# A four-layer graph network on one core: constants made inside the embedding, accumulators cleared by two engines, more tiles fetched row by row

## The chip, the cores and the metric

The kernel runs on one core of a Trainium2 chip. The metric is the device time of one execution in microseconds, as the median of several runs; lower is better. The core has TensorE (PE in the profile, PEld for its weight loads), VectorE (DVE), ScalarE (ACT), GpSimd (POOL) and SyncE (SP), which work in parallel and wait for each other by semaphores, and 16 DMA engines that all queues share.

## The reference

A graph has 6,250 nodes with 256 features and 106,250 directed edges, sorted by destination. Four layers follow each other, each on the normalized and rectified features, each added to its input:

```python
h = jnp.maximum(_layernorm(x), 0.0)
x = x + schnet(h, edge_index, edge_weight, edge_attr)   # msg = (h @ w1.T)[src] * filter(edge); sum by dst; two dense layers
h = jnp.maximum(_layernorm(x), 0.0)
x = x + gat(h, edge_index)                              # 8 heads: softmax over each node's in-edges, weighted sum of h[src]
h = jnp.maximum(_layernorm(x), 0.0)
x = x + mean(h, edge_index)                             # (h @ W + b)[src] summed by dst, divided by the degree
h = jnp.maximum(_layernorm(x), 0.0)
x = x + gcn2(h, edge_index)                             # two graph convolutions with batch norms, 64 and 2 wide
```

## The kernel before

The program is a row of stages; each is a `Phase` with its own buffers and semaphores, and at its end all engines meet in a barrier. Stages on nodes (`embed0`, `nodes_schnet`, `nodes_gat`, `nodes_mean`) go over 13 chunks of 512 nodes (4 tiles of 128). Stages on edges (`edges_schnet`, `edges_gat`, `edges_mean`, `edges_gcn`, `edges_pairs`) go over 832 tiles of 128 edges, in groups of four tiles. For each tile POOL issues one indirect DMA that gathers the source rows of its 128 edges from a table in memory; a one-hot matrix `sel` of the destinations within a window of 128 nodes is built; TensorE multiplies the rows by it into PSUM (`psa`), and DVE adds the result to an accumulator `acc` in SBUF, at a column that is read from the list of destinations. Each engine's program is written out in its own block, in the order in which the engine runs it; nothing is reordered.

- **`constants`**, the first stage: SP loads the index columns `src_sb`, `dst_sb` and `base_b`; POOL makes the identity `ident` and the counters; DVE makes `ones`, `eps`, `iota`, `part`, `pair`, and `rel` (destination less the tile's base). Everything ends before the next stage.
- **`embed0`**, the second stage: SP loads the weights `w`, then x by chunks into a ring of four. For each chunk DVE takes `statistics` (`BATCH_NORM_STATS2`, `BATCH_NORM_AGGREGATE`), ACT turns the variance into `rstd`, DVE normalizes (`n_norm`), TensorE transposes (L282) and projects (L329), ACT copies out (`hT`, `O`), POOL stores. `staggered` runs the steps so that in step s DVE takes the statistics of chunk s and normalizes chunk s-1. DVE also clears the accumulator of the next stage, in four pieces behind the statistics of chunks 1 to 4 (L455), and makes the `penalties`, six operations on 832 columns, ahead of chunk 3.
- **`edges_gat`** (attention): 52 iterations of 16 tiles, rows in a ring of three iterations (48 gathers). On ACT each iteration starts with the selections `sel_t` (L1236) and `copy_src` (`l_src_v`, L1283), which waits for all 16 gathers of its iteration. The accumulator has three planes of 6,656 columns; ACT clears them (L1228) behind a wait for all of DVE's setup (`setup`, 4), whose last instruction is `is_last` (L1342). DVE's first `add` waits for `acc_zero`.
- **`edges_mean`**: 208 groups, rows in a ring of eight groups. Of most groups POOL gathers four tiles (L1971). The last tile of some groups comes in one of two other ways: at `looks` (19 groups, every tenth) TensorE looks the rows up in a copy of the table in SBUF (L2096, in four rounds in the groups before); at `by_row` groups the queue of SP or of ACT fetches 128 single rows into `own` (L1919), two buffers for each queue. `asked[g]` is the number of tiles left to POOL. The schedule of `by_row` follows from `BY_ROW`:

```python
first_at, apart = 20, (GROUPS - 24) // BY_ROW
by_row = {g: h for h in range(2) for g in range(first_at + h * (apart // 2), first_at + h * (apart // 2) + apart * BY_ROW, apart)}
```

With 10 it gives each queue 10 groups, 18 apart, from group 20 (SP) and 29 (ACT). SP also loads, between its tiles, the rows from which the one-hots of the look-ups are made (`mixes`, L1940).

## Time and profile before

| | us |
|---|---|
| median of 3 runs | 5339.54 (5337.13 to 5340.34) |
| the profiled execution | 5341.28 |
| its span | 5339.3 |
| PE busy | 4632.9 (87%) |
| DVE busy | 3945.2 (74%) |
| POOL busy | 3383.1 (63%) |
| ACT busy | 1987.0 (37%) |

The span runs from the first to the last instruction that the profiler saw. Busy shares are averages over stages that have different limits, so they don't say what a change inside one stage is worth. Row times start at the span's start. A row "idle before <-releaser" says how long the engine had stood still ahead of the instruction and what ended that; "issue" is idle time for which the profile shows no cause. A row of a queue (SPq) gives the time over which its transfers were issued, not when they landed.

### The profile page before, as it was taken

How to read it: one execution, taken by the hardware profiler on the slowest of the kernel's cores; microseconds unless marked ns; L12 is line 12 of the kernel's file. 1: busy time of each engine (PE TensorE's matmuls, PEld its weight loads, DVE VectorE, ACT ScalarE, POOL GpSimd, SP SyncE). 2: the span in 40 equal slices, each digit the busy share in tenths (PEclk: the TensorE clock that was granted, in tenths of full speed). 3: DMA queues.
4: the chain of work that ended last, by engine and by line, in shares of the span. 5: the costliest groups of instructions: out<-in, count | busy, mean ns of one | idle time of the engine just before them, and what ended most of it. 6: DMA issues, size and time to landing. Idle time of an engine off the chain costs nothing. (4 is left out here: it accounts for less than half of the span.)

```text
span 5339.3 us, 107982 instructions
## 1 busy us (share of the span) xinstructions
PE 4632.9 (87%) x25603; PEld 3568.3 (67%) x25603; DVE 3945.2 (74%) x8645; ACT 1987.0 (37%) x3745; POOL 3383.1 (63%) x3489
## 2 busy tenths in 40 slices
PE   5999999999995888888885488888876899999793
PEld 4888888888775888888884466666655566666431
DVE  5999999999874888888788555555556677777673
ACT  3767666666534655555554200000003000000470
POOL 2677777777516767676640477777764777777473
PEclk8999999999996988888897799999987999999896
DMA  6333333333334555555535533333336111111243
GB/s 198 116 104 103 104 102 106 101 105 103 94 122 126 130 126 125 127 126 126 126 82 160 170 112 112 112 111 110 107 106 168 38 37 39 39 35 29 61 116 108
DMA packets 460843, 563.49 MB, mean 106 GB/s; under 512 B 213296, under 2 KB 331364, under 8 KB 460288
## 3 DMA queue, kind: packets, MB, share of 16 engines
q0 software_dynamic: 153728, 372.39, 25.9%
q1 hardware_dynamic: 292985, 173.79, 12.2%
q10 hardware_dynamic: 13640, 11.88, 0.9%
q8 instruction: 172, 2.82, 0.2%
q14 instruction: 318, 2.61, 0.2%
HBM read 505.12 MB, written 59.42 MB: 106 GB/s over the span
## 5 line engine op out<-in xcount | busy, mean ns | idle before, releaser
L507 POOL DMA_INDIRECT l_rows<-tmp_tab,l_idx x832 | 882.0, 1060 | 377.8 <-issue 252.2
L1217 POOL DMA_INDIRECT l_rows<-tmp_tab,src_sb x832 | 789.7, 949 | 335.0 <-issue 235.8
L1971 POOL DMA_INDIRECT l_rows<-tmp_tab,src_sb x793 | 749.8, 946 | 247.3 <-issue 236.6
L2267 POOL DMA_INDIRECT l_rows<-tmp_tab,src_sb x695 | 656.4, 944 | 235.5 <-issue 202.0
L805 PE MATMUL l_psw<-l_fw,l_ssp 128*128 128x256 f32 x3328 | 763.1, 382 | 0.0
L805 PEld LDWEIGHTS l_psw<-l_fw,l_ssp 128*128 128x128 f32 x3328 | 615.9, 190 | 154.0 <-issue 77.3
L1537 PE MATMUL l_psa<-l_sel,l_rows 128*128 128x128 f32 x3328 | 605.7, 311 | 52.4 <-DVE acc L1437 51.1
L2370 PE MATMUL l_found<-l_tabs,l_hot 128*128 128x384 f32 (+1 forms) x1872 | 650.6, 501 | 0.0
L1537 PEld LDWEIGHTS l_psa<-l_sel,l_rows 128*128 128x128 f32 x3328 | 511.9, 220 | 69.3 <-DVE acc L1437 56.1
L2118 PE MATMUL l_psa<-l_sel,l_rows 128*128 128x128 f32 x3248 | 436.7, 289 | 129.7 <-DVE l_sel L1983 48.6
L1437 DVE TENSOR_TENSOR acc<-acc,l_psa 128x384 f32 x832 | 460.5, 553 | 104.3 <-DVE acc L1430 9.8
L2118 PEld LDWEIGHTS l_psa<-l_sel,l_rows 128*128 128x128 f32 x3248 | 406.7, 200 | 186.6 <-issue 83.3
L2370 PEld LDWEIGHTS l_found<-l_tabs,l_hot 128*128 128x128 f32 x1872 | 347.4, 191 | 251.5 <-issue 66.1
L1993 DVE TENSOR_TENSOR acc<-acc,l_psa 128x256 f32 x832 | 350.0, 421 | 120.0 <-PE l_psa L2118 22.4
L818 PEld LDWEIGHTS l_psa<-l_sel,l_msg 128*128 128x128 f32 x3328 | 408.0, 192 | 15.7 <-issue 1.6
L2096 PE MATMUL l_found<-region,l_hot 128*128 128x512 f32 x950 | 416.1, 588 | 0.0
L818 PE MATMUL l_psa<-l_sel,l_msg 128*128 128x128 f32 x3328 | 412.5, 276 | 1.3 <-DVE acc L725 1.3
L656 ACT ACTIVATE l_mag<-l_psz,l_fb 128x512 f32<-128x512 f32 x416 | 261.7, 679 | 395.6 <-PE l_psz L792 395.6
L2456 ACT ACT_TABLE_LOAD x1 | 1.3, 1283 | 970.6 <-PEq L127 970.6
L1537 PE MATMUL l_psa<-l_sel,l_wx 128*128 128x128 f32 x1664 | 360.9, 303 | 0.0
L725 DVE TENSOR_TENSOR acc<-acc,l_psa 128x256 f32 x832 | 354.3, 426 | 1.7 <-DVE acc L725 0.6
L705 DVE TENSOR_TENSOR l_msg<-l_psw,l_fb 128x512 f32<-128x512 f32 x416 | 288.4, 694 | 89.8 <-issue 84.4
(368 smaller groups left out, 7962.1 us busy)
## 6 DMA issues: line engine op xcount, KB each, us to landing
l_rows<-tmp_tab,src_sb POOLq DMA_INDIRECT x2320
l_edge<-in_edge_t SPq DMA_DIRECT2D x104, 256.0 KB
l_own<-tmp_tab ACTq DMA_DIRECT2D x1280, 1.0 KB
l_own<-tmp_tab SPq DMA_DIRECT2D x1280, 1.0 KB
l_own<-tmp_tab ACTq DMA_DIRECT2D x1280, 0.2 KB
l_own<-tmp_tab SPq DMA_DIRECT2D x1280, 0.2 KB
tmp_x<-n_X SPq DMA_DIRECT2D x39, 512.0 KB
n_X<-in_x SPq DMA_DIRECT2D x26, 512.0 KB
```

The lines of the kernel that those rows point to most:

```text
L507: nc.gpsimd.indirect_dma_start(out=rows[r][:, t, :], out_offset=None, in_=table[:, :], in_offset=bass.IndirectOffsetOnAxis(ap=idx[q][:, j: ...
L725: nc.vector.tensor_tensor(a, a, psa[:, t * D:(t + 1) * D].rearrange("p (k r) -> p k r", k=KH), ALU.add).then_inc(added, 1)
L805: last = nc.tensor.matmul(psw[:, t * D:(t + 1) * D], ssp[b % 2][:, k, t * P:(t + 1) * P], fw2[:, k, :], start=(k == 0), stop=(k == KH - 1))
L818: last = nc.tensor.matmul(psa[:, t * D + k * P:t * D + (k + 1) * P], msg[b % 2][:, t, k * P:(k + 1) * P], sel[b][:, t, :], start=True, sto ...
L1217: nc.gpsimd.indirect_dma_start(out=rows[r][:, j, :], out_offset=None, in_=dram["tab1"][:, :], in_offset=bass.IndirectOffsetOnAxis(ap=sh["s ...
L1437: nc.vector.tensor_tensor(a, a, part, ALU.add).then_inc(added, 1)
L1537: last = nc.tensor.matmul(psa[:, col:col + P], left, sel[c.p][:, j, :], start=True, stop=True)
L1971: nc.gpsimd.indirect_dma_start(out=rows[g % ROWS][:, t, :], out_offset=None, in_=table[:, :], in_offset=bass.IndirectOffsetOnAxis(ap=sh["s ...
L2096: last = nc.tensor.matmul(found[:, k % 2 * 512:k % 2 * 512 + (top - lo) * D].rearrange("p (h n) -> p h n", n=D), hot[n % 2][:, j, :], tabs ...
L2118: last = nc.tensor.matmul(psa[:, at:at + P], left[:, k * P:(k + 1) * P], sel[b][:, t, :], start=True, stop=True)
L2267: nc.gpsimd.indirect_dma_start(out=rows[g % ROWS][:, t, :], out_offset=None, in_=table[:, :], in_offset=bass.IndirectOffsetOnAxis(ap=sh["s ...
L2370: last = nc.tensor.matmul(found_of(n)[:, 0:SPANS[j] * H3].rearrange("p (h n) -> p h n", n=H3), hot[n % BUFS][:, j, :], tabs[:, j:j + (SPAN ...
```

## The change

Three edits. First, the stage `constants` is gone, its work sits inside `embed0`: SP asks for chunk 0 of x first, then `w`; the index columns come in at chunk 6 and `rel` is made ahead of the statistics of chunk 9; `ones`, `iota`, `part`, `pair` ahead of chunk 2; the penalties move from chunk 3 to chunk 6; the accumulator is cleared in 13 pieces, one behind each normalize. Second, in `edges_gat` ACT clears two planes as its first instructions, and DVE clears the third behind its setup. Third, `BY_ROW` in `edges_mean` is 13 instead of 10: 13 groups for each queue, 14 apart, from group 20 (SP) and 27 (ACT).

```diff
@@ embed0, sync
-                sp.dma_start(w[:, :, :], by_half(dram["w1_t"])).then_inc(w_in, 16)
-
                 def step(at):
-                    if isinstance(at(0).n, int) and at(0).n == 2:
+                    if at(0).n == 6:
+                        sp.dma_start(sh["src_sb"][:, :], dram["src_cols"][:, :]).then_inc(cols_in, 16)
+                        sp.dma_start(sh["dst_sb"][:, :], dram["dst_cols"][:, :]).then_inc(cols_in, 16)
+                        sp.dma_start(base_b[:, :], dram["dst_cols"][0:1, :].broadcast_to([P, TILES])).then_inc(cols_in, 16)
+                    if at(0).n == 3:
                         for i in range(3):
                             sp.dma_start(runs[i][:, :], dram["dst_flat"][:, i:i + TILES * P].rearrange("a (p n) -> (a p) n", p=P)
...
                     sp.dma_start(nm.X[r][:, :, :], node_rows(dram["x"], c.n)).then_inc(x_in[r], 16)
+                    if c.n == 0:
+                        sp.dma_start(w[:, :, :], by_half(dram["w1_t"])).then_inc(w_in, 16)
@@ embed0, vector
+                def ranges():
+
+                    dve.wait_ge(made, 1)
+                    nc.vector.memset(sh["ones"][:, :], 1.0)
+                    nc.vector.tensor_copy(sh["iota"][:, :], iota_i[:, :])
+                    nc.vector.tensor_copy(sh["part"][:, :], part_i[:, :])
+                    nc.vector.tensor_scalar(pair_i[:, :], part_i[:, :], 1, None, ALU.logical_shift_right).then_inc(paired, 1)
+                    dve.wait_ge(paired, 1)
+                    nc.vector.tensor_copy(sh["pair"][:, :], pair_i[:, :])
+
+                def relative():
+
+                    dve.wait_ge(cols_in, 48)
+                    nc.vector.tensor_tensor(sh["rel"][:, :], sh["dst_sb"][:, :], base_b[:, :],
+                                            ALU.subtract).then_inc(rel_done, 1)
+
                 def step(at):
-                    if at(0) and isinstance(at(0).n, int) and at(0).n == 3:
+                    if at(0) and at(0).n == 2:
+                        ranges()
+                    if at(0) and at(0).n == 6:
                         penalties()
+                    if at(0) and at(0).n == 9:
+                        relative()
                     if at(0):
                         c = at(0)
                         dve.wait_ge(x_in[c.n % AHEAD], c.n // AHEAD * 16 + 16)
                         nm.statistics(dve, c)
-                        if isinstance(c.n, int) and 0 < c.n < PEEL:
-                            part = NW // (PEEL - 1)
-                            nc.vector.memset(acc[:, :, (c.n - 1) * part:c.n * part], 0.0).then_inc(cleared, 1)
                     if at(1):
                         nm.normalize(dve, at(1))
+                        c = at(1)
+                        part = NW // CHUNKS
+                        nc.vector.memset(acc[:, :, c.n * part:(c.n + 1) * part], 0.0).then_inc(cleared, 1)
@@ edges_gat, scalar
+                for k in range(KH):
+                    last = nc.scalar.activation(acc[:, k, :], sh["iota"][:, 0:1].to_broadcast([P, NW]), ACT.Copy)
+                last.then_inc(acc_zero, 1)
                 act.preload_act_table_set(EXP_LN)
                 act.wait_ge(setup, 4)
-                for k in range(PLANES):
-                    last = nc.scalar.activation(acc[:, k, :], sh["iota"][:, 0:1].to_broadcast([P, NW]), ACT.Copy)
-                last.then_inc(acc_zero, 1)
@@ edges_gat, vector
+                for k in range(KH, PLANES):
+                    nc.vector.memset(acc[:, k, :], 0.0).then_inc(tail_zero, 1)
                 dve.wait_ge(setup, 4)
...
                         dve.wait_ge(acc_zero, 1)
+                        dve.wait_ge(tail_zero, PLANES - KH)
@@ edges_mean
-    BY_ROW, PERIOD, FIRST, SLOTS = 10, 10, 20, 8
+    BY_ROW, PERIOD, FIRST, SLOTS = 13, 10, 20, 8
@@ bass_gnn_stack
-        constants(nc, dram, sh)
```

How DVE's instructions stand in the first chunks of the embedding before (`n_stats` and `n_mv` belong to statistics, `n_norm` to the normalize, `acc` is the accumulator of the next stage, the rows from L437 on are the penalties):

```order
L246 BN_AGGR n_mv<-n_stats 128x2 x4
L455 MEMSET acc 128x2x1664
L253 TENSOR_SCALAR n_norm<-n_X,n_mv,n_rstd 128x256 x4
L242 BN_STATS n_stats<-n_X 128x6 x4
L246 BN_AGGR n_mv<-n_stats 128x2 x4
L455 MEMSET acc 128x2x1664
L253 TENSOR_SCALAR n_norm<-n_X,n_mv,n_rstd 128x256 x4
L437 TENSOR_TENSOR n_base_r<-n_runs,n_base_r 128x832
L439 CAST n_rel_b<-n_base_r 128x832
L441 TENSOR_TENSOR n_cut<-n_runs 128x832
```

and at the same place now, from the statistics of chunk 1 on:

```order
L245 BN_AGGR n_mv<-n_stats 128x2 x4
L252 TENSOR_SCALAR n_norm<-n_X,n_mv,n_rstd 128x256 x4
L447 MEMSET acc 128x2x512
L419 MEMSET ones 128x128
L420 CAST iota<-n_iota_i 128x128
L421 CAST part<-n_part_i 128x1
L422 TENSOR_SCALAR n_pair_i<-n_part_i 128x1
L424 CAST pair<-n_pair_i 128x1
L241 BN_STATS n_stats<-n_X 128x6 x4
L245 BN_AGGR n_mv<-n_stats 128x2 x4
L252 TENSOR_SCALAR n_norm<-n_X,n_mv,n_rstd 128x256 x4
L447 MEMSET acc 128x2x512
```

The memset stands behind the normalize and is a third of its old size; the penalties are three chunks further on.

ACT at the start of attention before, from the stage's entry to the first selections and the copy of the gathered source values (one wait for DVE's setup stands behind the table load):

```order
L1225 ACT_TABLE_LOAD
L1228 ACTIVATE acc<-iota 128x6656 x3
L1236 ACTIVATE l_sel_t<-l_rel_b,l_minus 128x512
L1241 ACTIVATE l_sel_t<-l_sel_t 128x512
L1236 ACTIVATE l_sel_t<-l_rel_b,l_minus 128x512
```

and now:

```order
L1222 ACTIVATE acc<-iota 128x6656 x2
L1224 ACT_TABLE_LOAD
L1232 ACTIVATE l_sel_t<-l_rel_b,l_minus 128x512
L1237 ACTIVATE l_sel_t<-l_sel_t 128x512
L1232 ACTIVATE l_sel_t<-l_rel_b,l_minus 128x512
```

Two of three clears stand ahead of the load and of the wait; the third is now DVE's.

POOL in the mean layer before, groups 20 to 29 (x3 is a group of which the last tile comes another way):

```order
L1971 DMA l2_rows4<-tmp_tab2,src_sb 128x256 x3
L1971 DMA l2_rows5<-tmp_tab2,src_sb 128x256 x3
L1971 DMA l2_rows6<-tmp_tab2,src_sb 128x256 x4
L1971 DMA l2_rows7<-tmp_tab2,src_sb 128x256 x4
L1971 DMA l2_rows0<-tmp_tab2,src_sb 128x256 x4
L1971 DMA l2_rows1<-tmp_tab2,src_sb 128x256 x4
L1971 DMA l2_rows2<-tmp_tab2,src_sb 128x256 x4
L1971 DMA l2_rows3<-tmp_tab2,src_sb 128x256 x4
L1971 DMA l2_rows4<-tmp_tab2,src_sb 128x256 x4
L1971 DMA l2_rows5<-tmp_tab2,src_sb 128x256 x3
```

and now, groups 20 to 28:

```order
L1970 DMA l2_rows4<-tmp_tab2,src_sb 128x256 x3
L1970 DMA l2_rows5<-tmp_tab2,src_sb 128x256 x3
L1970 DMA l2_rows6<-tmp_tab2,src_sb 128x256 x4
L1970 DMA l2_rows7<-tmp_tab2,src_sb 128x256 x4
L1970 DMA l2_rows0<-tmp_tab2,src_sb 128x256 x4
L1970 DMA l2_rows1<-tmp_tab2,src_sb 128x256 x4
L1970 DMA l2_rows2<-tmp_tab2,src_sb 128x256 x4
L1970 DMA l2_rows3<-tmp_tab2,src_sb 128x256 x3
L1970 DMA l2_rows4<-tmp_tab2,src_sb 128x256 x4
```

ACT's first tile moves from group 29 to group 27; over the stage POOL issues 787 gathers instead of 793.

## Rows read from the trace of the kernel before

**Rows 1.** Groups of instructions by line: busy us, mean ns | idle us before, releasers

```profile
L1217 POOL DMA_INDIRECT l_rows<-tmp_tab,src_sb x832 | 789.7, 949 | 335.0 <-issue 235.8 <-PE l_psa L1537 90.2 <-POOLq L147 9.0
...
L1971 POOL DMA_INDIRECT l_rows<-tmp_tab,src_sb x793 | 749.8, 946 | 247.3 <-issue 236.6 <-POOLq L147 5.9 <-PE l_psa L2118 4.9
```

**Rows 2.** Timeline from the start: start us, us, instruction [idle before <-releaser]

```profile
0.73 0.41 SPq L348 DMA_DIRECT2D src_sb<-in_src_cols  x1
...
6.27 1.03 DVE L375 TENSOR_TENSOR rel<-dst_sb,const_base_b 128x832 f32<-128x832 int32 x1 [4.54 <-DMA const_base_b<-in_dst_cols]
...
9.29 1.01 SPq L416 DMA_DIRECT2D n_X<-in_x  x2
...
13.27 1.41 DVE L242 BATCH_NORM_STATS2 n_stats<-n_X 128x6 f32<-128x256 f32 x4 [5.98 <-DMA n_X<-in_x]
...
15.61 1.41 DVE L242 BATCH_NORM_STATS2 n_stats<-n_X 128x6 f32<-128x256 f32 x4 [0.41 <-DMA n_X<-in_x]
```

**Rows 3.** Timeline, embedding, chunks 1 to 4, DVE

```profile
28.47 1.02 DVE L437 TENSOR_TENSOR n_base_r<-n_runs,n_base_r 128x832 int32<-128x832 int32 x1
...
33.16 1.40 DVE L242 BATCH_NORM_STATS2 n_stats<-n_X 128x6 f32<-128x256 f32 x4
...
38.48 1.20 DVE L253 TENSOR_SCALAR n_norm<-n_X,n_mv,n_rstd 128x256 f32<-128x256 f32 x4
...
42.16 2.83 DVE L455 MEMSET acc<- 128x3328 f32 x1 [0.64 <-issue]
```

**Rows 4.** Timeline, start of the layer after: a memset beside gathers

```profile
4080.94 1.34 DVE L2320 MEMSET l_dst_l<- 128x1536 int32 x1 [0.27 <-issue]
...
4081.81 0.94 POOL L2267 DMA_INDIRECT l_rows<-tmp_tab,src_sb  x1 [0.30 <-issue]
```

**Rows 5.** Timeline, embedding, chunks 5 to 12

```profile
54.88 1.04 PE L282 MATMUL n_psT<-ident,n_norm 128*128 128x128 f32 x8
...
74.04 1.60 DVE L253 TENSOR_SCALAR n_norm<-n_X,n_mv,n_rstd 128x256 f32<-128x256 f32 x4 [0.89 <-ACT n_rstd L264]
...
85.18 1.04 PE L282 MATMUL n_psT<-ident,n_norm 128*128 128x128 f32 x8
```

**Rows 6.** Timeline, start of the attention layer (gathers 16, 32 and 48)

```profile
1650.53 17.03 ACT L1228 ACTIVATE acc<-iota 128x6656 f32<-128x6656 f32 x3 [12.54 <-DVE l_is_last L1342]
...
1657.88 0.95 POOL L1217 DMA_INDIRECT l_rows<-tmp_tab,src_sb  x1 [0.30 <-issue]
...
1673.81 0.29 ACT L1283 ACTIVATE l_src_v<-l_rows 128x128 f32<-128x128 f32 x1
...
1677.86 0.95 POOL L1217 DMA_INDIRECT l_rows<-tmp_tab,src_sb  x1 [0.30 <-issue]
...
1688.55 0.31 ACT L1283 ACTIVATE l_src_v<-l_rows 128x128 f32<-128x128 f32 x1
...
1697.89 0.95 POOL L1217 DMA_INDIRECT l_rows<-tmp_tab,src_sb  x1 [0.30 <-issue]
...
1706.83 0.31 ACT L1283 ACTIVATE l_src_v<-l_rows 128x128 f32<-128x128 f32 x1
...
1728.96 0.31 ACT L1283 ACTIVATE l_src_v<-l_rows 128x128 f32<-128x128 f32 x1 [0.22 <-issue]
```

**Rows 7.** Timeline, mean layer: SP queue, and TensorE at the first fetched tile

```profile
3046.97 63.58 SPq L1919 DMA_DIRECT2D l_own<-tmp_tab  x128
...
3112.73 63.57 SPq L1919 DMA_DIRECT2D l_own<-tmp_tab  x128
...
3112.41 2.90 PE L2118 MATMUL l_psa<-l_sel,l_rows 128*128 128x128 f32 x12 [6.76 <-DMA l_own<-tmp_tab]
```

**Rows 8.** Timeline, end of the mean layer

```profile
3958.08 2.05 PE L2118 MATMUL l_psa<-l_sel,l_rows 128*128 128x128 f32 x16 [0.54 <-DVE l_sel L1983]
...
3981.61 0.94 POOL L1971 DMA_INDIRECT l_rows<-tmp_tab,src_sb  x1 [0.30 <-issue]
...
3984.40 2.02 PE L2118 MATMUL l_psa<-l_sel,l_rows 128*128 128x128 f32 x16 [1.45 <-issue]
```

More of the change, by code:

```diff
@@ L43 @@
 NP = CHUNKS * CN
-PEEL = 5
 PAD_DST = 6300
@@ L463, in _ @@
                 act.preload_act_table_set(EXP_LN)
+                act.wait_ge(eps_done, 1)
                 def step(at):
@@ L483, in step @@
                         c = at(1)
+                        if c.n == 0:
+                            pe.wait_ge(w_in, 16)
                         pe.wait_ge(nm.hT_done, c.n + 3)
```

57 lines of the change are left out of this document (16 added, 41 removed).

## Prediction

> **What bounds the kernel now.** The program is a row of stages with a barrier after each, so a microsecond saved inside a stage reaches the end whole, unless the same stage gives it back. The chain that ended last only tells of the last stage; I therefore read each of the three stages that the change touches by itself: first the groups by line for who waits for whom, then the timeline around each edit.
>
> Mean layer: GpSimd (POOL) issues 793 gathers, 749.8 us busy plus 247.3 us idle in front of them, of which only 4.9 us were spent waiting for TensorE to free a buffer [rows 1]. POOL never really waits: 1.25 us per gather set the length of the layer. At its end this is plain: TensorE starts a group 1.85 us after that group's last gather was issued (3981.61 + 0.94 to 3984.40) and then waits for the next [rows 8]. Attention layer: the same instruction, 832 times, but with 90.2 us of waiting for `psa` matmuls (57 waits) [rows 1]. POOL needs 16 x 1.25 = 20.0 us for an iteration, an iteration takes somewhat more: the compute engines set the pace, POOL has some 8% to spare. Embedding: from chunk 5 to chunk 12 the transposes start at 54.88 and 85.18, 4.33 us per chunk [rows 5], while VectorE (DVE) has idle time; ahead of that DVE's memsets and penalties stretch the chunks [rows 3].
>
> **Part 1, constants inside the embedding.** What goes: the stage `constants`. Its first transfer is issued at 0.73, its last DVE instruction ends at 6.27 + 1.03 = 7.30, and the first rows of x are asked for at 9.29 only [rows 2]. Now they are the first transfer of the program. It stands behind the one barrier that the transfer at 0.73 stood behind, and five semaphore increments of POOL that no row shows; their cost lies between nothing and the whole step from 7.30 to 9.29, 2.0 us. I take 0.4, as most of that step is the end of a stage, which is gone: x is asked for at 1.1 (0.73 to 2.7), 8.2 us earlier. Chunk 0 lands 4.0 us after it is asked for (13.27 - 9.29), chunk 1 after 6.3 (15.61 - 9.29) [rows 2]; the weights now stand between them instead of ahead, half a us more, so statistics of chunk 1 start at 7.9.
>
> The DVE work changes too. Four memsets of 2x1664 become thirteen of 2x512. A row gives 2.83 us for 3,328 elements, and an idle gap of 0.64 us ahead that nothing released [rows 3]; a memset of 1,536 has 1.34 and 0.27 [rows 4]. The gap grows with the size, so I count it as memset: 3.47 and 1.61, a slope of 1.04 ns per element, which gives 1.61 - 512 x 0.00104 = 1.08 us for 1,024. By the durations alone it would be 0.87. The Trainium skill ("VectorE: DVE Perf Modes", section "Zero memsets can be issued as uint32 (trn2)") says that a memset takes one cycle per element whatever its type; at the 0.96 GHz of its specifications that is an estimate of 3.47 us for 3,328, so by that rule the trace's duration is short by just the gap and the two together agree. For thirteen memsets the rule makes 13.9 us, the durations alone 11.3.
>
> From statistics of chunk 1 to transposes of chunk 5 it was 54.88 - 15.61 = 39.3 us [rows 2, 5]. Take out four memsets (13.9), put in five small ones (5.4) and the five small operations on iota and part (0.9: the penalties' six operations on 832 elements take 33.16 - 28.47 = 4.7 us [rows 3], and these have 128 elements or fewer): 31.7. The penalties stay in this stretch, three chunks later. TensorE now has less slack in the stretch, whose early matmuls are slower, so I add 1.4: transposes of chunk 5 at 7.9 + 31.7 + 1.4 = 41.0 (bounds 39.6 and 43). From there on two paces compete. TensorE's is 4.33. DVE's is 42.16 - 0.64 - 38.48 = 3.04 without a memset [rows 3], 4.12 with it, and 4.52 where the normalize takes 1.60 instead of 1.20 [rows 3, 5], as it does in all steady chunks, where POOL issues a store beside it. Seven chunks at 4.33 to 4.52 and once the subtraction of `rel` (1.03): 31.3 to 32.7. I take 32.1: transposes of chunk 12 at 73.1, against 85.18. All behind them (last projection, stores) is as before. Part 1: **-12.1 us**, bounds -8 (only the earlier start) and -14. The transfers of src, dst and base go in at chunk 6; `rel` is needed by chunk 9's step, over 12 us later, three times what chunk 0 needed to land. That cover hides them; without it DVE would stand for some 4 us.
>
> **Part 2, accumulators of attention.** Before, ScalarE (ACT) first waits until DVE's setup is over and starts three clears at 1650.53, which take 17.03 us; its first selections follow at 1667.5 and `src_v` of iteration 0 at 1673.81 [rows 6]. Now ACT does two planes (2 x 5.7 us) while DVE does its setup, ended by 1650.5, and DVE clears the third plane behind it: 6,656 elements, 6.9 us by the slope, until 1657.5, with nothing queued behind it on DVE but scans that wait for `src_v`. So ACT is free 16.5 us earlier, and `src_v` of iteration 0 could run at 1657.2. But it needs the gathers of its iteration, and POOL's start doesn't move. The 16th, 32nd and 48th gather are issued by 1658.83, 1678.81 and 1698.84 [rows 6]; each lands 1.85 us later [rows 8], so `src_v` can't run before 1660.7, 1680.7 and 1700.7. It ran at 1673.81, 1688.55 and 1706.83: the gain shrinks from 13.1 to 7.9 to 6.1. Iteration 3 came 22.1 us after that (1728.96 [rows 6]), its gathers pass every 20.0: compute is then the slower again and keeps the 6.1. With a TensorE that has its full clock a bit earlier, 6.5. Part 2: **-6.5 us**; bounds -3 (gathers that land late) and -8.5.
>
> Would the memset slow the gathers? Beside the memset at 4080.94 the gather at 4081.81 took 0.94 us [rows 4], as it does without one; I count nothing. A rule of the Trainium skill speaks against this ("SBUF — State Buffer", "Who interferes with whom"): DVE and GpSimd share a port pair as an exclusive lock, and a DVE operation in a two-port mode keeps POOL from writing gather descriptors.  The same page leaves one-input operations outside the two-port modes free of the lock, which by that rule is this case; the trace agrees.
>
> **Part 3, 13 row-fetched tiles on each queue.** Six gathers fewer on POOL: 6 x 1.25 = 7.5 us, if the rows are there. SP needs from one tile's first row to the next tile's 3112.73 - 3046.97 = 65.8 us, 63.6 of it row transfers [rows 7]; with a second one-hot load in the turn 0.45 more. Before, a tile was due on each queue every 18 groups, some 86 us. Now it is every 14 groups: 56 tiles less 3.4 that aren't gathered, 52.6 x 1.25 = 65.8. SP is exactly as fast as it must be. Its first tile was late, TensorE waited 6.76 us until 3112.41, 1.9 us behind the last row [rows 7]; from then on SP stays as late (12 turns of 65.8 plus 3 extra loads: last tile 3112.4 + 791 = 3903.4). So TensorE reaches that tile's group at least 7 us behind the gathers, more than before. Twenty groups follow, at 5.0 us by POOL (4 x 1.25) and 2.05 + 0.54 = 2.6 by TensorE without look-ups [rows 8]; the last seven or so have none, enough to catch up some 15 us. Buffers are eight groups deep, so POOL isn't stopped. ACT's turns are one us shorter than SP's. Part 3: **-7.0 us**, bounds -2 and -7.5.
>
> **Sum.** -12.1 - 6.5 - 7.0 = -25.6. The profiled execution took 5341.28 us (span 5339.3), so the changed one would take 5315.7 in such an execution; the median of before is 1.7 lower, and so is my number: 5314.
>
> **Rivals.**
> - *Attention gives it back.* If the memset of 6.9 us holds up POOL's gathers, the 48th is issued at 1705.7 and `src_v` of iteration 2 can't run before 1707.6, later than its old 1706.83: part 2 is gone, 5314 + 6.5 = 5320.5. For it: that `src_v` has no slack behind the gathers [rows 6]. Against: the gather beside a memset [rows 4]. (The page rule that would bring it about is the port lock of "SBUF — State Buffer" in the Trainium skill, if the memset ran in a two-port mode.) With half of part 1 missing as well, because DVE's 4.52 and late x chunks rule the embedding, 5324. Chance 0.17.
> - *Two parts out of three come to nothing*: gain under 10.7 us, 5329 to 5350. That needs, say, the mean layer to end no earlier, since TensorE doesn't catch up behind SP's last tile, and attention as above. Chance 0.07.
> - *SP becomes the bound of the mean layer*: the one that ends slower. A turn of 65.8 us has no slack; from the point where it is longer than 65.8 + 15/12 = 67 us each further us costs 12. At 70 us (row transfers at 0.53 us instead of 0.50, for instance because ACT's queue now issues all the time) it is +36 against -7.5: 5358. Against: 63.6 us for SP's 128 rows was measured while ACT was issuing too. Chance 0.04.
> - *More than forecast*: embedding at TensorE's pace and the start at 0.73, attention 8.5: under 5307. Chance 0.08.
>
> My forecast (5307 to 5320) has 0.64. Within 0.2% (10.7 us, about what a measurement of this kernel can tell from no change) is the second rival and a slice of others: 0.08; slower 0.04; faster 0.88. The range 5306 to 5325 leaves out the two middle rivals' far ends and the slow one.
>
> **What would show it.** Right: first statistics near 5 us, transposes of chunk 12 near 73, the first gather of the first edge stage some 12 us earlier; ACT's first selection in attention 16 us earlier relative to the stage's first gather and the last `src_v` 6 to 7 us earlier; 787 gathers in the mean layer, which is 7 us shorter, with waits of TensorE for `own` every 14 groups. Wrong: POOL waiting for `psa` in the mean layer, SP turns over 67 us, gathers stretched beside the memset at the start of attention, or a DVE step over 4.6 us in the embedding.

## The result, and the profile after

The changed kernel takes **5300.02 us** (5299.47 to 5301.71, 3 runs) against 5339.54: ratio 0.9928, 95% interval 0.9914 to 0.9941. Forecast were 5314.0, range 5306 to 5325. Sign and two of three sizes were right (parts 1 and 3), that of part 2, the attention layer, was not, and the time lies below the range. Measured once more, in five runs beside ten of before, the ratio was 0.9935 (0.9921 to 0.9948), 5301.75 against 5336.49: 35 to 40 us faster, where 25.5 were forecast.

Where the microseconds came from, by the first and last instruction of each stage in the two profiled executions (shift of that instruction's start against before, us):

| up to | shift | of it in this stage | forecast |
|---|---|---|---|
| transposes of the embedding's chunk 12 | -14.3 | -14.3 | -12.1 |
| last add of the first edge stage | -16.7 | -2.4 | 0 |
| first gather of attention | -17.2 | -0.4 | 0 |
| last add of attention | -34.4 | **-17.3** | -6.5 |
| first gather of the mean layer | -33.8 | +0.7 | 0 |
| last add of the mean layer | -41.4 | -7.6 | -7.0 |
| last add of the program | -40.6 | +0.8 | 0 |

The miss is the attention layer. The groups by line answer to [rows 1]: six gathers fewer in the mean layer, still without a wait for TensorE that matters; in attention POOL waits 69.6 us for `psa` instead of 90.2.

```profile
L1213 POOL DMA_INDIRECT l_rows<-tmp_tab,src_sb x832 | 791.5, 951 | 315.4 <-issue 236.8 <-PE l_psa L1536 69.6 <-POOLq L146 9.0
...
L1970 POOL DMA_INDIRECT l_rows<-tmp_tab,src_sb x787 | 744.1, 945 | 246.0 <-issue 234.0 <-POOLq L146 6.1 <-PE l_psa L2117 5.9
```

The timeline of the embedding, which answers to [rows 2, 3, 5]:

```profile
1.36 0.44 SPq L376 DMA_DIRECT2D n_X<-in_x  x1
5.49 1.41 DVE L241 BATCH_NORM_STATS2 n_stats<-n_X 128x6 f32<-128x256 f32 x4 [3.98 <-DMA n_X<-in_x]
7.70 1.41 DVE L241 BATCH_NORM_STATS2 n_stats<-n_X 128x6 f32<-128x256 f32 x4 [0.28 <-DMA n_X<-in_x]
...
15.76 0.91 DVE L447 MEMSET acc<- 128x1024 f32 x1 [0.16 <-issue]
16.59 1.34 DVE L241 BATCH_NORM_STATS2 n_stats<-n_X 128x6 f32<-128x256 f32 x4
...
38.84 1.10 PE L281 MATMUL n_psT<-ident,n_norm 128*128 128x128 f32 x8 [3.66 <-DVE n_norm L252]
39.77 5.31 PE L328 MATMUL n_psO<-n_w,n_hT 128*128 128x256 f32 x16
44.91 1.04 PE L281 MATMUL n_psT<-ident,n_norm 128*128 128x128 f32 x8
45.79 3.62 PE L328 MATMUL n_psO<-n_w,n_hT 128*128 128x256 f32 x16
...
70.89 1.04 PE L281 MATMUL n_psT<-ident,n_norm 128*128 128x128 f32 x8
```

x is asked for at 1.36 and the statistics of chunk 1 start at 7.70 (forecast 1.1 and 7.9). A memset of 1,024 elements shows as 0.91 with 0.16 of idle "issue" ahead (forecast 1.08 together). Transposes of chunk 5 start at 38.84, 2.2 us earlier than forecast; from there to chunk 12 it is 32.05 us (forecast 32.1). The first of these seven steps takes 6.07 us: behind its wait of 3.66 us TensorE projects at a granted clock of 0.68 (5.31 us for what takes 3.62 at 1.00). The other six take TensorE's 4.33 each, and `rel`, made at 49.35, delays none of them.

The start of the attention layer, which answers to [rows 6]:

```profile
1619.57 11.39 ACT L1222 ACTIVATE acc<-iota 128x6656 f32<-128x6656 f32 x2 [18.78 <-PEq L146]
...
1627.16 1.36 POOL L1213 DMA_INDIRECT l_rows<-tmp_tab,src_sb  x1 [0.30 <-issue]
...
1634.23 5.61 DVE L1340 MEMSET acc<- 128x6656 f32 x1 [1.34 <-issue]
...
1637.78 0.95 POOL L1213 DMA_INDIRECT l_rows<-tmp_tab,src_sb  x1 [0.30 <-issue]
...
1644.53 0.31 ACT L1279 ACTIVATE l_src_v<-l_rows 128x128 f32<-128x128 f32 x1 [5.15 <-DMA l_rows<-tmp_tab,src_sb]
...
1664.62 0.31 ACT L1279 ACTIVATE l_src_v<-l_rows 128x128 f32<-128x128 f32 x1 [7.06 <-DMA l_rows<-tmp_tab,src_sb]
...
1684.86 0.31 ACT L1279 ACTIVATE l_src_v<-l_rows 128x128 f32<-128x128 f32 x1 [4.26 <-DMA l_rows<-tmp_tab,src_sb]
...
1704.84 0.31 ACT L1279 ACTIVATE l_src_v<-l_rows 128x128 f32<-128x128 f32 x1 [3.49 <-DMA l_rows<-tmp_tab,src_sb]
...
1724.75 0.31 ACT L1279 ACTIVATE l_src_v<-l_rows 128x128 f32<-128x128 f32 x1 [2.41 <-DMA l_rows<-tmp_tab,src_sb]
```

As far as `src_v` the mechanism is the forecast one: it now waits for gathers, 2.0 us behind the last of each iteration (forecast 1.85), and DVE's memset (5.61 and 1.34 of gap, forecast 6.9 together) slows no gather: 0.95 beside it. It is beside DVE's setup, some us earlier, that gathers take 1.36. But at `src_v` the wait for gathers doesn't stop at iteration 2: 1704.84 and 1724.75 are still 20 apart. From `src_v` of iteration 2 to that of iteration 8 the windows read, before and then after (columns: stretch; us; busy time of PE, PEld, DVE, ACT, POOL; granted clock; DMA share; GB/s), with iterations 10 to 51 as second row:

```profile
1706.83:1834.49 127.66, 111.43 (x853) 107.83 (x854) 104.56 (x229) 75.91 (x206) 93.81 (x100) 0.90 0.54 131
1880.30:2764.76 884.46, 762.63 (x5823) 736.89 (x5824) 716.05 (x1559) 519.99 (x1396) 611.89 (x647) 0.89 0.52 125
```

```profile
1684.86:1805.74 120.88, 103.29 (x817) 99.69 (x817) 100.84 (x223) 75.83 (x204) 91.32 (x97) 0.93 0.55 135
1853.16:2729.72 876.56, 753.99 (x5824) 728.37 (x5825) 715.25 (x1559) 518.83 (x1396) 614.34 (x649) 0.90 0.52 126
```

By `src_v` the gain is 5.6 us at iteration 2 (counted from the end of the 16th gather; 6.1 forecast), and it seems to grow by 6.8 in the next six iterations. But `src_v` is ACT's, and ACT can run ahead of TensorE: the first window before holds 853 matmuls and the one after only 817. TensorE takes the `src_v` of an iteration with one matmul, `val_ps`. Those of iterations 2 and 8, and the windows between the two, before:

```profile
1713.69 0.33 PE L1475 MATMUL l_val_ps<-ident,l_src_v 128*128 128x128 f32 x1
...
1840.17 0.33 PE L1475 MATMUL l_val_ps<-ident,l_src_v 128*128 128x128 f32 x1
```

```profile
1713.69:1840.17 126.48, 110.25 (x853) 106.65 (x852) 104.60 (x228) 75.90 (x205) 92.26 (x98) 0.91 0.53 131
```

and after:

```profile
1685.22 0.33 PE L1474 MATMUL l_val_ps<-ident,l_src_v 128*128 128x128 f32 x1 [0.42 <-ACT l_src_v L1279]
...
1812.70 0.33 PE L1474 MATMUL l_val_ps<-ident,l_src_v 128*128 128x128 f32 x1
```

```profile
1685.22:1812.70 127.48, 110.25 (x852) 106.61 (x852) 105.50 (x230) 76.20 (x206) 96.40 (x103) 0.91 0.55 134
```

Before, TensorE took `src_v` of iteration 2 only 6.9 us after it ran (1713.69 against 1706.83), as it was busy with earlier iterations; now it waits for it and takes it at once. So TensorE is 12.2 us earlier there, not 5.6. From there to iteration 8 it has the same work at the same granted clock and takes 127.5 us instead of 126.5: it gains nothing in these iterations. What changes in them is ACT's lead over TensorE: it grows from 0.4 to 7.0 us now and was 6.9 and 5.7 us before. Against the end of the 16th gather TensorE is 9.1 us earlier at iteration 1, 12.2 at 2, 11.0 at 3, 11.1 at 8 and 10.8 at 10.

So the layer gained in two places: 10.8 us up to iteration 10, all of it there by iteration 2, and 7.6 in the 41 later iterations, in which nothing was changed. The first 16 gathers took 0.8 longer, as they do in profiles without part 2 too, and the end of the layer 0.4.

In the mean layer SP is as fast as it must be: turns of 65.4 to 66.1 us, and TensorE waits for the fetched rows in six places, 38.8 us in all, without stopping POOL. SP's queue and TensorE, answering to [rows 7]:

```profile
3081.98 63.44 SPq L1918 DMA_DIRECT2D l_own<-tmp_tab  x128
3147.61 63.36 SPq L1918 DMA_DIRECT2D l_own<-tmp_tab  x128
...
3081.81 2.90 PE L2117 MATMUL l_psa<-l_sel,l_rows 128*128 128x128 f32 x12 [9.56 <-DMA l_own<-tmp_tab]
```

### The profile page after: what moved, and what is told of

It reads as the page before. It is cut to its first block and busy times, and to the rows that moved or that the text cites. A ratio compares the mean times of both kernels' runs of the same rounds, so it can differ in the third digit from the quotient of the medians.

```text
span 5299.7 us, 110332 instructions
## 1 busy us (share of the span) xinstructions
PE 4618.3 (87%) x25603; PEld 3553.1 (67%) x25603; DVE 3948.1 (74%) x8655; ACT 1979.7 (37%) x3744; POOL 3379.1 (64%) x3483
## 3 DMA queue, kind: packets, MB, share of 16 engines
q1 hardware_dynamic: 293759, 174.19, 12.1%
## 5 line engine op out<-in xcount | busy, mean ns | idle before, releaser
L503 POOL DMA_INDIRECT l_rows<-tmp_tab,l_idx x832 | 883.5, 1062 | 375.5 <-issue 253.1
L1536 PE MATMUL l_psa<-l_sel,l_rows 128*128 128x128 f32 x3328 | 598.9, 308 | 55.4 <-DVE acc L1436 52.8
L2117 PE MATMUL l_psa<-l_sel,l_rows 128*128 128x128 f32 x3224 | 429.9, 287 | 144.0 <-DVE l_sel L1982 49.9
L1536 PEld LDWEIGHTS l_psa<-l_sel,l_rows 128*128 128x128 f32 x3328 | 504.3, 217 | 72.5 <-DVE acc L1436 58.5
L2117 PEld LDWEIGHTS l_psa<-l_sel,l_rows 128*128 128x128 f32 x3224 | 399.1, 198 | 202.2 <-DVE l_sel L1982 91.8
L1992 DVE TENSOR_TENSOR acc<-acc,l_psa 128x256 f32 x832 | 349.7, 420 | 123.7 <-PE l_psa L2117 25.3
L721 DVE TENSOR_TENSOR acc<-acc,l_psa 128x256 f32 x832 | 342.9, 412 | 1.7 <-DVE acc L721 0.6
```

The source lines that it names most:

```text
L503: nc.gpsimd.indirect_dma_start(out=rows[r][:, t, :], out_offset=None, in_=table[:, :], in_offset=bass.IndirectOffsetOnAxis(ap=idx[q][:, j: ...
L1536: last = nc.tensor.matmul(psa[:, col:col + P], left, sel[c.p][:, j, :], start=True, stop=True)
L1992: nc.vector.tensor_tensor(a, a, p, ALU.add).then_inc(added, 1)
L2117: last = nc.tensor.matmul(psa[:, at:at + P], left[:, k * P:(k + 1) * P], sel[b][:, t, :], start=True, stop=True)
```

## Experiments

Two theories for attention. A: the clears are worth 17 us, fixed. B: they are worth about 10, and the rest is where TensorE's dips to the low clock fall. The expectations count iterations at `src_v`, and so does the text below unless it names TensorE: "it. 2 to 8" is the time between the `src_v` of these iterations, "0 to 10" counts from the end of the 16th gather, and a dip iteration is one of iterations 10 to 50 that took under 23 us at a granted clock below 0.9 (those above are turns of the loop and, rarely, an iteration with a longer stretch at the low clock).

**One part at a time.** The kernel before with one of the three parts, and the changed kernel without part 2. The edits are the three hunks of the change, each by itself.

> The kernel before with part 1 alone (constants inside the embedding, 13 memsets). Theory A (each part has a fixed gain, and the 17 us of the attention layer belong to the clears): 14 us less than before up to the first edge stage, nothing anywhere else, 5325. Theory B (the clears bring about 10 us, and the remaining 7 to 8 us of the attention layer, like 2.5 us of the first edge stage, come from where TensorE's clock dips fall, which any shift of the start changes): also 14 at the start, but the first edge stage and the attention layer each differ by some us from their length before, with either sign; 5315 to 5333.

> The kernel before with part 2 alone (ACT clears two planes first, DVE the third). Theory A: 17 us, all of it in the attention layer, 5322. Theory B: 10 us are there by iteration 9, as in the changed kernel, with the iterations 2 to 8 at POOL's 20.0 us; what comes behind iteration 9 is another number than the changed kernel's 7 to 8 us: 5324 to 5332.

> The kernel before with part 3 alone (13 fetched tiles on each queue). Both theories: the mean layer is 7.0 to 7.5 us shorter, nothing before it moves; 2 us may be given back or gained in the stages behind it, 5331 to 5334.

> The changed kernel with the clears of the attention layer as before (all three on ACT behind the setup). Theory A: 17 us more than the changed kernel, 5317; the attention layer has its old length to within 1 us. Theory B: the attention layer is shorter or longer than in the kernel before by some us although nothing in it is changed, and the total lies 8 to 20 us above the changed kernel, 5308 to 5320.

Measured beside 23 runs of before at 5338.06: part 1 alone 5323.22 (ratio 0.9974, 0.9963 to 0.9985), part 2 alone 5328.94 (0.9982, 0.9973 to 0.9991), part 3 alone 5331.70 (0.9989, 0.998 to 0.9998), parts 1 and 3 5315.64 (0.9962, 0.9949 to 0.9976). That is -14.8, -9.1, -6.4; part 2 comes out at 9 us alone and at some 14 on top of the others. The intervals of the two overlap (5 to 14 for the first; the second is a difference of two programs, each known to some 7 us), so the times don't show that they differ. A falls: 17 us lies outside the first. B agrees with these times, though one expectation of A came true as well: without part 2 the layer has its old length (1167.5 for 1168.1). Two more things: the first edge stage, untouched and unshifted in the profiles of parts 2 and 3 alone, is 3.0 and 2.8 us shorter in them than in the profile before, so its -2.4 is no effect of the change. And the embedding has more than one outcome: of eleven profiles with the same new embedding the last transpose starts at 70.5 to 71.7 in five and at 73.4 to 73.8 in six, by two waits for `rstd`, of at most 1.3 us in the five and of 1.6 to 2.1 in the six; before it is 85.9. The forecast of -12.1 is that of the six.

**The same kernel again, and later clears.**

```diff
@@ third plane on ACT (two planes later: range(1), and range(1, PLANES) behind the wait)
                 for k in range(KH):
                     last = nc.scalar.activation(acc[:, k, :], ...)
-                last.then_inc(acc_zero, 1)
                 act.preload_act_table_set(EXP_LN)
                 act.wait_ge(setup, 4)
+                for k in range(KH, PLANES):
+                    last = nc.scalar.activation(acc[:, k, :], ...)
+                last.then_inc(acc_zero, 1)
...
-                for k in range(KH, PLANES):
-                    nc.vector.memset(acc[:, k, :], 0.0).then_inc(tail_zero, 1)
```

> The changed kernel once more, unaltered. The attention layer took 1150.8 us in its profile (first gather to last add), 1157.3 with part 2 alone, and 1164.5 to 1168.1 in four profiles without part 2. If the 6.5 us between the first two belong to the single execution, this profile has another length than 1150.8, up to 1157, and the iterations 10 to 51 take something between 876 and 885 us; the time is then between 5299 and 5306. If they belong to the combination of the parts, both numbers come back to within 1 us, and the time is 5299 to 5302.

> The changed kernel, but ACT clears the third plane too, behind the wait for the setup; DVE clears nothing. ACT idles 5.15 us ahead of src_v of iteration 0 in the changed kernel, so the 5.7 us come out as 0.6 us there and are gone at iteration 1, which the gathers hold back: same time as the changed kernel to within its scatter, and the gathers of the first 20 us as long as there (the memset beside them costs nothing). The rival, that DVE's memset is worth something by itself or slows the gathers: src_v of iteration 1 and 2 earlier or later by over 1 us relative to the first gather.

> The changed kernel, but only one plane is cleared ahead of the setup, two (11.4 us) behind it, all on ACT. src_v of iteration 0 comes 6.3 us later (8.3 us behind its gathers). Theory gather-bound: iterations 0 and 1 are short ones (14.7 and 18.2 us where nothing holds them back), so src_v of iteration 1 stands 3.0 us behind its gathers and that of iteration 2 at 2.0 again, iterations 2 to 8 run at 20.0, and the time is that of the changed kernel to within its scatter. The rival, that a later start is carried to the end: 6 us more.

Again: 5301.75, and the profile repeats (210.6 and 877.4 us for 0 to 10 and 10 to 51, against 210.7 and 876.6). A third profile of the same attention code, that with `BY_ROW` 14 below, has 210.5 and 877.4. So the short late iterations are no accident of one execution: they belong to this program. Third plane on ACT: 5309.14 (0.9946, 0.9932 to 0.996), 7.4 us more than the changed kernel, whose time was expected. Iterations 0 to 10 take 210.8, as expected; the 7 us that the layer lost lie all behind iteration 10 (883.5), where the two programs have the same instructions. Two planes later: 5312.1 (0.9953, 0.994 to 0.9967), 10.4 us more, where again the changed kernel's time was expected. ACT's timeline shows what was expected of the first iterations:

```profile
1634.53 11.39 ACT L1225 ACTIVATE acc<-iota 128x6656 f32<-128x6656 f32 x2 [6.25 <-DVE l_is_last L1339]
1652.17 0.29 ACT L1280 ACTIVATE l_src_v<-l_rows 128x128 f32<-128x128 f32 x1
1666.91 0.31 ACT L1280 ACTIVATE l_src_v<-l_rows 128x128 f32<-128x128 f32 x1
1686.21 0.31 ACT L1280 ACTIVATE l_src_v<-l_rows 128x128 f32<-128x128 f32 x1 [1.35 <-DMA l_rows<-tmp_tab,src_sb]
```

8.1 us behind the gathers, then 2.8, then 2.1 with a wait: at `src_v` the late start is absorbed by iteration 2. But iterations 2 to 8 then took 126.2 us and not 120: that half of the expectation failed. TensorE's matmuls say why. TensorE takes `src_v` of iteration 2 at 1689.00, without a wait and 2.2 us later against the gathers than in the changed kernel, and is 1.9 us later at iteration 10. So some 2 of the 6 us of later start stay; only ACT stood at the gathers.

**A pause ahead of the layer.**

```diff
+            pause(nc, sh, 16)        # a stage in which ACT writes 128x16 (long: 128x6656) to a buffer of its own
             edges_gat(nc, dram, sh, acc)
```

> The changed kernel with a small stage of its own ahead of the attention layer, in which ACT writes 16 columns to a buffer that nothing reads (a pause of some 5 us for all engines). Profiles so far: from src_v of iteration 10 to that of iteration 51 the changed kernel takes 876.6 to 877.4 us (three profiles of the same code up to there) with 5 iterations whose granted clock is below 0.9, the kernel before 884.5 and 884.7 with 10. If the number of such iterations follows from when the layer starts against something outside it (theory phase), it is another than 5 here, and the 41 iterations take 880 to 886 us. If it follows from the layer's own code and its first iterations alone, it stays 5 and 877 us, and the kernel is slower by the pause and nothing else.

> The same with 6,656 columns, a pause 5.7 us longer. Theory phase: a third value, between 876 and 886 us for the iterations 10 to 51, not ordered by the length of the pause. The other theory: 877 us and 5 iterations again, total 5.7 us above the short pause.

> The kernel before with the long pause. Theory phase: the iterations 10 to 51 take another time than 884.5 us, more likely less, as 10 slow iterations are the most seen so far. The other theory: 884.5 us and 10 such iterations. In both, iterations 0 to 10 take 220.5 to 221.5 us, since nothing makes their start earlier: that is what the changed clears are worth 10 to 11 us against.

Measured 5312.19, 5318.25 and 5346.62 (beside 5338.01). Windows of iterations 2 to 8 and 10 to 51, first the short pause, then the long one:

```profile
1688.24:1810.99 122.75, 106.10 (x832) 102.29 (x830) 101.10 (x224) 76.03 (x205) 92.88 (x99) 0.91 0.54 135
1858.38:2741.87 883.49, 760.90 (x5824) 733.56 (x5825) 715.20 (x1559) 520.15 (x1396) 612.51 (x647) 0.90 0.51 125
```

```profile
1693.73:1816.02 122.29, 105.51 (x826) 101.71 (x827) 100.67 (x223) 76.12 (x205) 92.42 (x99) 0.92 0.54 134
1860.11:2745.71 885.60, 762.90 (x5823) 735.63 (x5824) 715.22 (x1559) 520.25 (x1395) 616.08 (x650) 0.89 0.52 125
```

The same attention code takes 883.5 and 885.6 us where it took 877, with seven dip iterations instead of five. The times agree: the short pause itself costs 1 us at most (187.8 us from the last add of the first edge stage to attention's first gather, against 186.8 and 188.3 in the changed kernel's two profiles), yet all five runs (5310.12 to 5316.1) lie above all of the changed kernel (up to 5305.24). So what stands ahead of the layer does change it. That it does so by the moment at which the layer starts (theory phase) is not shown: with `BY_ROW` 14 its first gather comes 2.0 us later than in the changed kernel's profile and it keeps 877.4; with the short pause it comes 2.7 us later and takes 883.5. For the kernel before the pause tells little: 883.4 instead of 884.5, though of another make (11 dip iterations, turns of the loop of 26.0 us instead of 23.8).

The profiles together (layer: first gather to last add; low: us at the low clock in iterations 10 to 51, from windows of one iteration each, as 2 x (1 - granted clock) x length):

| program | it. 0 to 10 | 10 to 51 | low | dip iterations | layer |
|---|---|---|---|---|---|
| before | 221.5 | 884.5 | 191 | 10 | 1168.1 |
| part 1 alone | 221.0 | 880.1 | 177 | 7 | 1164.5 |
| part 3 alone | 220.8 | 884.7 | 193 | 10 | 1167.8 |
| parts 1 and 3 | 220.5 | 883.3 | 182 | 7 | 1167.5 |
| before, pause | 221.2 | 883.4 | 182 | 11 | 1167.8 |
| **changed** | 210.7 | 876.6 | 170 | 5 | 1150.8 |
| changed, again | 210.6 | 877.4 | 174 | 5 | 1151.0 |
| part 2 alone | 210.4 | 883.3 | 190 | 8 | 1157.3 |
| changed, short pause | 213.3 | 883.5 | 183 | 7 | 1160.2 |
| changed, long pause | 208.9 | 885.6 | 188 | 7 | 1157.9 |
| changed, memsets on POOL | 207.3 | 876.6 | 175 | 7 | 1147.0 |

The five without part 2 average 1167.1 us for the layer, the five different ones with it (without "again") 1154.6: part 2 is worth 12.5 us on the mean. Most of it lies before iteration 10 (210.1 against 221.0, 10.9 us; 215.7 against 226.8 by TensorE's matmul), 2.1 behind it (881.1 against 883.2), and 6 us more or less in any one program go with where the dips fall. But for the changed kernel each row is one execution, and that of part 2 alone took 5333.29 us, 4.4 above the median of its program.

**The embedding without DVE's memsets.**

```diff
                def step(at):
+                    nc.gpsimd.memset(acc[:, :, c.n * part:(c.n + 1) * part], 0.0).then_inc(cleared, 1)
                     store_out(nc, pool, ph, O, dram["tab0"], c, o_done, stored)
```

> The changed kernel with the 13 memsets of the embedding on POOL, ahead of its stores. In the changed kernel a chunk costs DVE 4.13 us where nothing holds it up, 0.99 of it the memset. If DVE sets the pace of the embedding there, a chunk falls to the 4.33 of TensorE or below and the transposes of chunk 12 come 2 to 8 us earlier than 70.9. If the prediction's TensorE pace of 4.33 is a floor that the changed kernel has reached already (4.55 per chunk from chunk 5 to 12, with the subtraction and one wait for rstd in it), it is 1.5 us at most. Against both: POOL and DVE writing SBUF at once could stretch the normalizes, and the gain would be nil.

5299.89 beside 5338.01 (0.9927, 0.9914 to 0.9941), the changed kernel's time: nothing gained (in the profiles the embedding is 2.8 us longer and attention 3.8 shorter). Taking 12.9 us (13 x 0.99) off DVE did not make the embedding shorter; chunk 12's transposes come at 73.71. A row of the groups of the changed kernel, and then the same here:

```profile
L252 DVE TENSOR_SCALAR n_norm<-n_X,n_mv,n_rstd 128x256 f32<-128x256 f32 x52 | 19.0, 427 | 3.5 <-ACT n_rstd L263 3.5
```

```profile
L252 DVE TENSOR_SCALAR n_norm<-n_X,n_mv,n_rstd 128x256 f32<-128x256 f32 x52 | 28.2, 602 | 7.5 <-ACT n_rstd L263 7.5
```

9.2 us of the 12.9 went into stretched normalizes (602 ns instead of 427), 4 into waits for `rstd`. The two penalties of `tensor_scalar` show how, one beside a memset and one alone:

```profile
33.53 1.64 DVE L421 TENSOR_SCALAR n_cut<-n_cut 128x832 f32<-128x832 f32 x1
33.74 0.97 POOL L396 MEMSET acc<- 128x1024 f32 x1
...
36.12 0.59 DVE L421 TENSOR_SCALAR n_cut<-n_cut 128x832 f32<-128x832 f32 x1
```

The first is longer by as much as the memset lasts. So this run can't tell what DVE's memsets cost the embedding; that DVE is not the bound in the later chunks stands on the changed kernel's own rows, where TensorE has six steps of 4.33 us without a wait.

**One fetched tile more.** `BY_ROW` 14 instead of 13.

> The changed kernel with 14 fetched tiles on each queue, a tile due every 13 groups: 52 tiles less about 3.4, 60.8 us of POOL, where a turn of SP takes 65.8. By the sum of the prediction SP falls 5 us further behind at each of 13 turns: its last tile is there some 972 us after the layer's first gather, 19 groups follow at 2.6 to 3 us by TensorE, and POOL is stopped by full buffers: the layer takes 1020 to 1030 us instead of 992, the kernel 5328 to 5338. If SP had slack: 1.5 us... 2 us faster than the changed kernel (two gathers fewer).

5354.99 (1.0032, 1.0019 to 1.0046): slower than before. The mean layer takes 1041.9 us, more than the 1020 to 1030 expected (5328 to 5338 for the kernel). POOL and TensorE in the groups by line:

```profile
L1970 POOL DMA_INDIRECT l_rows<-tmp_tab,src_sb x785 | 742.5, 946 | 297.3 <-issue 232.5 <-PE l_psa L2117 58.8 <-POOLq L146 6.1
```

```profile
L2117 PE MATMUL l_psa<-l_sel,l_rows 128*128 128x128 f32 x3216 | 430.2, 288 | 187.8 <-DMA l_own<-tmp_tab 98.7 <-DVE l_sel L1982 40.5 <-DVE acc L1992 22.7
```

SP's turns are 65.8 us as before, where a tile is due every 60.8; TensorE waits for fetched rows in ten places, 98.7 us in all, and POOL 58.8 for buffers. 13 is the last number that fits.

**What the dips hang on.** TensorE's timeline of the changed kernel around `src_v` of iteration 31, at the place where it waits for `lrelu`:

```profile
2296.05 0.63 PE L1536 MATMUL l_psa<-l_sel,l_rows 128*128 128x128 f32 x4
...
2299.55 0.20 PE L1500 MATMUL l_psm<-ident,l_lrelu 128*8 128x1 f32 x2 [1.70 <-DVE l_lrelu L1398]
...
2300.46 1.22 PE L1536 MATMUL l_psa<-l_sel,l_rows 128*128 128x128 f32 x4 [0.66 <-DVE acc L1436]
...
2301.90 1.06 PE L1536 MATMUL l_psa<-l_sel,l_rows 128*128 128x128 f32 x4
```

The same four matmuls take 0.63 us ahead of the wait and 1.06 behind it: the clock has gone from 2.4 to 1.2 GHz. This comes once in nearly every iteration, for 3 to 4 us; a dip iteration has more of it. Over 490 iterations of the 14 profiles other than those of the next three kernels (10 to 50 without the loop's six turns, counted from one `val_ps` matmul of TensorE to the next) the best straight line is 19.3 us + 0.45 us per us at the low clock; no iteration is more than 0.7 us off it. So an iteration of compute has no fixed length, and a little under half of the time at the low clock is lost. Three kernels fill the wait, with work moved there (the last `expand`), in the changed kernel and in the one before, or with work that means nothing:

```diff
                         edge_maxima(m)
+                    if c:
+                        expand(c, 3)
+                    if m:
                         falls(m)
                     if a:
                         windows(a, 3)
-                    if c:
-                        expand(c, 3)
@@ gap filled, instead of the move
                         edge_maxima(m)
+                        for i in range(6 if c else 0):
+                            nc.tensor.matmul(att_bank[:, SH + i * 64:SH + (i + 1) * 64], ident, ident[:, 0:64], ...)
                         falls(m)
```

> The changed kernel, with the last expand of an iteration (8 matmuls, 0.9 us) moved into the gap in which TensorE waits 1.7 us for lrelu. Both theories: an iteration of compute is 0.85 us shorter, from 20.8 to about 20.0 where nothing else changes, which is also what POOL needs for its gathers; 46 iterations or more gain 0.8, so the layer is 30 to 40 us shorter (1110 to 1120 us instead of 1150.8), the kernel 5260 to 5272. Theory that the low clock follows from the gap: with the gap at 0.8 us the dips get shorter or vanish, compute falls under 20.0 and the whole layer runs at the gathers' pace, src_v 2 us behind them, 1075 to 1090 us. Theory that the dips come by themselves at their own times: as many us at the low clock per iteration as now (3.3 to 3.8), src_v some 8 to 11 us behind the gathers.

> The kernel before with the same move. If compute is then no slower than the gathers, part 2 of the change loses its value behind iteration 2: against e9 it is slower by parts 1 and 3 (14 + 7.5) and by 0 to 8 us for the attention layer, 22 to 30 us in all, instead of 38.

> The changed kernel with 6 matmuls of 64 columns of the identity, written to a part of PSUM that nothing reads, in the gap in which TensorE waits 1.7 us for lrelu; nothing is moved and nothing gets shorter by them. Theory that the low clock follows from the gap: the 3.3 us at the low clock per iteration go, and with them up to 0.5 x 3.3 = 1.7 us per iteration, down to the 20.0 of the gathers: the layer is 30 us or more shorter. The other theory: nothing gets faster; the same 170 to 200 us at the low clock in iterations 10 to 51, and the same 877 to 886 us, or longer, if the fill delays the matmul behind it.

Expand moved: **5278.37** (4 runs; ratio to before 0.989, 0.9874 to 0.9905), 23 us below the changed kernel. The move in the kernel before: 5312.74 (0.9953, 0.9939 to 0.9967). Gap filled: 5309.13 (0.9948, 0.9935 to 0.9962). Two rows of TensorE's timeline with the move:

```profile
2287.26 1.03 PE L1522 MATMUL l_att_ps<-l_win,l_sel_t 128*128 128x8 f32 x8
2289.13 0.20 PE L1500 MATMUL l_psm<-ident,l_lrelu 128*8 128x1 f32 x2 [0.84 <-DVE l_lrelu L1398]
...
2291.62 1.06 PE L1536 MATMUL l_psa<-l_sel,l_rows 128*128 128x128 f32 x4
```

The wait fell from 1.70 to 0.84 and the dip still comes. The layer takes 1128.7 us, 22 less; 30 to 40 were expected (5260 to 5272 for the kernel). The gap filled, windows of iterations 2 to 8 and 10 to 51, and then of 2 to 8 by TensorE's matmul:

```profile
1686.23:1806.29 120.06, 106.49 (x903) 103.10 (x903) 101.87 (x225) 76.38 (x204) 90.83 (x97) 0.99 0.55 136
1851.79:2742.39 890.60, 799.22 (x6316) 776.86 (x6317) 715.75 (x1559) 520.76 (x1396) 614.62 (x651) 0.91 0.51 125
```

```profile
1686.74:1809.34 122.60, 109.03 (x925) 105.62 (x924) 104.20 (x229) 76.60 (x205) 92.75 (x98) 0.99 0.55 136
```

With the wait filled the granted clock of iterations 2 to 8 is 0.99 instead of 0.93 (0.91 by TensorE's windows), so there the dip does hang on the idle time. `src_v` stands at the gathers as before, six times 20.0; TensorE gets through its six iterations in 122.6 us instead of 127.5, 4.9 less for some 20 us less at the low clock. Behind iteration 10 dips are back (0.91), and the 41 iterations are longer than with the gap. This profile is of one of the two slowest of five runs (5316.53 and 5316.68; the other three took 5304.4 to 5309.13), so how much longer they are on the whole is not shown; the median lies 7.4 us above the changed kernel's. Neither theory holds for the whole layer.

The move in the kernel before takes 1138.2 us for the layer, 9.5 more than with parts 1 to 3, where 0 to 8 were expected (34.4 us more for the kernel, where 22 to 30 were): part 2 keeps its value when compute is faster. It lies before iteration 10 again (214.8 against 206.8 us, 860.0 against 858.3 behind).

## Why the prediction was right or wrong

- **Start of the embedding** (-8.2): right, -7.9. The 0.4 us for the first barrier was 0.6.
- **Embedding's stretch to chunk 5**: 38.84 instead of 41.0. The 1.4 us added for a TensorE with less slack was not there: the stretch took 31.1 us, below even the 31.7 without it, and at its end TensorE waited 3.66 us for DVE. The small operations took 0.5 us, not 0.9. The memsets were right (and by the durations alone, the slope of the same two rows gives 0.91 us, as measured, and not the 0.87 of the text).
- **From chunk 5 to chunk 12**: 32.05 for 32.1, by luck. The sum had seven steps of 4.33 to 4.52 and 1.0 us for `rel`. The rows have one step of 6.07, at the low clock behind the wait, six of 4.33, and nothing for `rel`. As the six profiles with late transposes have a first step of some 7.0 to 7.2 us, the -12.1 that they confirm is in part luck too; the changed kernel's own profile has -14.3.
- **Part 2, `src_v` of the first three iterations**: right, 5.6 us for 6.1; clears and memset held up no gather.
- **The failed step** is to take this for the gain of the layer: "the gain shrinks from 13.1 to 7.9 to 6.1", and "compute is then the slower again and keeps the 6.1". That compute is the slower again is right: TensorE takes 21.1 us an iteration before and 21.2 after. But what compute keeps is its own gain, and its pace is that of TensorE (and of DVE, for which TensorE waits in every iteration), not of ACT. Before, TensorE took `src_v` of iteration 2 at 1713.69, 6.9 us after ACT had made it. Set against that row, the sum's own bound by the gathers (1700.7) leaves 12 to 13 us, not 6.1. Measured are 12.2 at iteration 2 and 10.8 at iteration 10; the mean over five kernels each is 11.1. The term should have been -10 to -12.
- **The further 7 us** that the changed kernel's profile shows over part 2 alone are three dip iterations fewer at 1.3 us each (22.1 against 20.8), and one iteration of 23.9 us at a granted clock of 0.79 that only the latter has. The prediction held the clock pattern fixed and put no spread on it. The pauses show that the same code has 877 or 884 us for these iterations by what stands ahead of it; what in that decides it, and why it repeats from run to run of the changed kernel, stays open.
- **Part 3**: right (-7.6 for -7.0), as was its reasoning that SP has no slack at 13 tiles, though TensorE waited for SP's rows in six places and not at every tile; at 14 the layer loses 49 us.
- **Rivals**: the memset holding up gathers did not happen. Its sum for half of part 1 missing as well is off: 5320.5 + 6 = 5326.5, not 5324, and so just outside the range. "More than forecast" did happen. Of the ways that it names, the embedding's came near (-14.3 for the bound of -14), with the start at 1.36 and not at 0.73; its 8.5 us for attention was too near, as it too was counted at `src_v`.

The Trainium skill, "TensorE: Matmul & The Clock Gate" (Part 1: The HAM clock gate), says that the hardware which sets TensorE's clock by its activity runs free of the program, so that where a program meets it shifts from case to case. The pauses agree with that for the changed kernel (877.4 against 883.5 and 885.6 us), without showing that it is the cause. That a profile repeats to 0.8 us is not explained by it.

## What to carry to other kernels

Read a gain at the engine that sets the pace, in the kernel before as in the one after. An engine that runs ahead of it shows too little where it had a lead (5.6 us at ACT's `src_v`, 12.2 at TensorE's matmul for the same iteration), and then a growing gain where only its lead grows; a window that holds fewer matmuls than its counterpart gives this away. Take TensorE's low clock as time, 0.45 of it lost here, and put a spread of its size (here 6 us in a 1150 us layer) on every forecast for code behind a shifted start. To learn what one edit is worth, measure it in more than one surrounding; the profiled layers gave 10.8 and 16.7 us for the same one here.

## What the runs showed of the hardware

- A memset on POOL slows `tensor_scalar` on DVE by its whole length: on 832 columns 1.64 us beside a memset of 0.97, 0.59 alone; the normalizes went from 427 to 602 ns on the mean. No `tensor_tensor` stood beside one. The Trainium skill, "SBUF — State Buffer" (Who interferes with whom), has copies and `tensor_scalar` contend with GpSimd for the shared port pair where their operands allow the two-port modes; the rows agree.
- Gathers issued beside DVE's setup of the attention layer took 1.36 to 1.55 us instead of 0.95, also beside `tensor_tensor` on 832 columns alone (the 1.55 at 1632.16 beside `is_last`, 1631.89 to 1632.90); those beside its memset of 6,656 elements took 0.95.
- 1.7 us without work in 20 are followed by 3 to 4 us at 1.2 GHz in nearly every iteration. With the gap filled the dip was nearly gone in iterations 2 to 8 (granted clock 0.99) and came back later (0.91).
